# A graph layer's edge loop: its first eight blocks in another order, its store waits moved behind the barrier, and its last stage in one block with it

## What is computed

```python
pre_u = jnp.einsum('bud,dk->buk', h_t, W1[:d])
pre_v = jnp.einsum('bvd,dk->bvk', h_t, W1[d:])
hidden = jax.nn.relu(pre_u[:, :, None, :] + pre_v[:, None, :, :] + b1)
S = jax.nn.sigmoid(jnp.einsum('buvk,ko->buvo', hidden, W2)[..., 0] + b2[0])
a_t = jnp.einsum('buv,bud->bvd', S * A_a, h_t)
m_t = jnp.einsum('uv,bud->bvd', A_m, h_t) * h_t
z_t = beta1 * h_t + beta2 * (jnp.einsum('bvd,de->bve', a_t, Wa) + ba) + beta3 * (jnp.einsum('bvd,de->bve', m_t, Wm) + bm)
```

## Time and profile before

| | us |
|---|---|
| median of 3 runs | 3447.57 |
| lowest, highest | 3445.82, 3448.07 |
| profiled execution | 3449.29 |
| its span, first to last instruction | 3447.2 |
| TensorE busy | 3356.6 |
| VectorE busy | 2841.7 |
| ScalarE busy | 2342.5 |
| GpSimd busy | 1836.9 |

### The profile page before, as it was taken

One profiled execution on the slowest core, in us unless ns is written; L12 is line 12 of the kernel. 1 busy time (PEld: TensorE's weight loads), 2 busy tenths in 40 slices (PEclk: granted clock), 3 DMA queues, 4 the chain that ended last, 5 costly groups with the idle time before them and its releaser, 6 DMA issues. The chain is left out here.

```text
span 3447.2 us, 56125 instructions
## 1 busy us (share of the span) xinstructions
PE 3356.6 (97%) x14230; PEld 2618.5 (76%) x14230; DVE 2841.7 (82%) x4857; ACT 2342.5 (68%) x14070; POOL 1836.9 (53%) x2379
## 2 busy tenths in 40 slices
PE   7999999999998999999999999999999999689999
PEld 5667667676666888778878888878878888578888
DVE  5566765766547999999999999999999999469897
ACT  1222121221116999899999999999999999688997
POOL 3221221221114667656666676666666665578886
PEclk9999999999999999999999999999999999899999
DMA  7876777767669656775675666666656647587775
GB/s 273 296 262 240 264 255 247 284 248 256 230 205 225 155 122 165 165 171 139 139 174 132 176 137 159 171 152 153 168 141 168 155 114 189 183 285 249 263 257 193
DMA packets 345402, 685.80 MB, mean 199 GB/s; under 512 B 38990, under 2 KB 252856, under 8 KB 323512
## 3 DMA queue, kind: packets, MB, share of 16 engines
q1 hardware_dynamic: 289088, 594.50, 59.6%
q0 software_dynamic: 21504, 53.31, 5.0%
q10 hardware_dynamic: 34480, 34.34, 2.9%
HBM read 444.01 MB, written 256.18 MB: 203 GB/s over the span
## 5 line engine op out<-in xcount | busy, mean ns | idle before, releaser
L1240 ACT ACTIVATE junk<-psum_a 128x128 f32<-128x128 f32 x6144 | 1611.5, 293 | 199.0 <-PE psum_a L1144 110.2
L1240 ACT ACTIVATION_READ_ACCUMULATOR junk<-psum_a 128x1 f32 x6144 | 1367.8, 224 | 0.0
L1185 DVE TENSOR_REDUCE group_sum<-psum_d 128x56 f32<-128x896 f32 x1024 | 1111.5, 1085 | 87.8 <-PE psum_d L1144 42.0
L1144 PE MATMUL psum_d<-v_t,pk 128*128 128x512 f32 x1920 | 754.6, 393 | 0.0
L1292 POOL DMA_INDIRECT sum_dram<-total,idx_all x512 | 506.9, 990 | 228.3 <-POOL total L1303 124.1
L996 POOL TENSOR_TENSOR own<-whole 128x256 f32<-128x256 f32 x128 | 126.0, 985 | 753.9 <-DVE own_mixed L789 420.3
L1143 PE MATMUL psum_d<-u_t,pk 128*128 128x512 f32 x1280 | 503.9, 394 | 5.8 <-issue 4.7
L689 PE MATMUL wide<-shared,h 128*128 128x512 f32 x1024 | 482.2, 593 | 0.0
L747 ACT COPY whole<-ring 128x256 f32<-128x256 f32 x128 | 47.7, 373 | 630.4 <-PE ring L661 630.4
L1144 PE MATMUL psum_a<-v_t,pk 128*128 128x512 f32 x1152 | 453.4, 394 | 0.0
L1604 ACT ACTIVATE masked<-masked,of_u,half_sign 128x128 f32<-128x128 f32 x1024 | 399.7, 480 | 61.7 <-POOL masked L1541 61.7
(11 more groups left out here) (225 smaller groups left out, 5532.8 us busy)
## 6 DMA issues: line engine op xcount, KB each, us to landing
rows_dram<-split SPq DMA_DIRECT2D x128, 512.0 KB, 3.2
sum_dram<-zero SPq DMA_DIRECT2D x128, 512.0 KB, 4.0
u_t<-rows_dram SPq DMA_DIRECT2D x64, 1024.0 KB
shared<-sum_dram SPq DMA_DIRECT2D x64, 1024.0 KB, 6.3
first_u<-rows_dram SPq DMA_DIRECT2D x62, 1024.0 KB
pk<-pick_dram SPq DMA_DIRECT2D x448, 128.0 KB
whole_dram<-whole SPq DMA_DIRECT2D x128, 256.0 KB, 3.4
pick_dram<-first_v SPq DMA_DIRECT2D x128, 256.0 KB, 3.0
```

Source lines behind the costliest of these rows:

```text
L1144: return nc.tensor.matmul(dst, pk[n % PKS][:, SLOTS + at:SLOTS + at + P], part(v_t[n % VG][:], b, LB), start=False, stop=True)
L1185: nc.vector.tensor_reduce(out_[:, :, 1:EG], in_[:, :, GW:LATE].rearrange("p b (g k) -> p b g k", k=GW), AX, ALU.add, apply_absolute_value= ...
L1240: last = nc.scalar.activation(junk[:, a % RING_A, k * LATE:(k + 1) * LATE], psum_a[a % RING_A][:, k * LATE:(k + 1) * LATE], ACT.Abs, accum ...
```

## The change

1. **Store waits.** SP's waits for the first stage's stores are taken out of that stage. They stand, as `stage_stored`, at the start of the edge loop on SP, DVE, ACT and POOL (and of the multi-pass code); PE has none. All engines wait for `passes_made` instead, load `passes_i`, meet at the barrier, and branch over the multi-pass code, which now stands between first stage and edge loop.
2. **First blocks.** `steps` orders the first eight blocks as (u, v) = (0, 0), (0, 1), (1, 0), (1, 1), (0, 2), (0, 3), (1, 2), (1, 3). SP loads `v_t1`, `u_t1`, `v_t2`, `v_t3` in this order, and the third u-tile at n = 6 instead of n = 4.
3. **One block.** Edge loop and last stage are functions of one block: each engine goes from one into the other without a barrier. SP waits for all scatters and then loads; PE waits for all `drained`. `of_u` is finished on DVE after the second-last block.
4. **Work ahead.** The four adds of steps k = 0 and 1 are made by POOL after the scatters of blocks 251 to 254, into `masked_ahead`, which takes the place of the second `hWa` tile in `shared`. `adj_first` is loaded ahead too. `hWa_all[1]` is now the first load of the last stage.

```diff
@@ end of the first stage
-                    sp.wait_ge(linear_stored, 16 * 2)
-                    sp.wait_ge(own_stored, 16)
-                    sp.wait_ge(hWa_stored, 16 * B)
-                    sp.wait_ge(base_stored, 16 * B)
-                    for i in range(RPK):
-                        sp.wait_ge(pick_stored[i], 16 * ((PAIRS - i + RPK - 1) // RPK))
+                    sp.wait_ge(passes_made, 1)
...
+            passes = nc.values_load(passes_i[0:1, 0:1], min_val=0, max_val=PASSES)
             nc.all_engine_barrier()
@@ order and buffers
-        blocks = [(k % ST, (k - TURN * jj) // ST % NGRP * VG + jj) for k in range(ST * NGRP) for jj in range(VG)]
+        steps = [(0, 0), (0, 1), (1, 0), (1, 1), (0, 2), (0, 3), (1, 2), (1, 3)]
+        steps += [(k, jj) for k in range(2, ST * NGRP) for jj in range(VG)]
+        first_of = [min(n for n, step in enumerate(steps) if step[0] == k) for k in range(ST * NGRP)]
+        def block_at(k, jj):
+            return k % ST, (k - TURN * jj) // ST % NGRP * VG + jj
+        blocks = [block_at(*step) for step in steps]
-        hWa_ahead = [shared[:, i * ROW:(i + 1) * ROW].rearrange("p (b d) -> p b d", d=D) for i in range(RAW)]
+        hWa_ahead = shared[:, 0:ROW].rearrange("p (b d) -> p b d", d=D)
+        masked_ahead = [shared[:, ROW + i * P * B:ROW + (i + 1) * P * B].rearrange("p (b v) -> p b v", v=P) for i in range(RAW)]
@@ new: the waits for the stores
+        def stage_stored(eng):
+            eng.wait_ge(linear_stored, 16 * 2)
+            eng.wait_ge(own_stored, 16)
+            eng.wait_ge(hWa_stored, 16 * B)
+            eng.wait_ge(base_stored, 16 * B)
+            for i in range(RPK):
+                eng.wait_ge(pick_stored[i], 16 * ((PAIRS - i + RPK - 1) // RPK))
+            for i in range(RW):
+                eng.wait_ge(rows_stored[i], 32 * ((B * NT - i + RW - 1) // RW))
@@ SP in the edge loop
+                stage_stored(sp)
                 for n in range(1, PKS - 1):
                     load_pick(n)
-                    if n < VG:
-                        load_v(0, n)
+                    if n == 2:
+                        load_u(1)
+                    elif n in (1, 4, 5):
+                        load_v(0, max(n - 2, 1))
...
-                        if n % VG == 0 and n // VG + 1 < n_blk // VG:
+                    if n == 6:
+                        load_u(2)
+                    if n % VG == 0 and n >= 2 * VG and n // VG + 1 < n_blk // VG:
                         load_u(n // VG + 1)
...
                         for t in range(RAW):
                             sp.dma_start(raw[t], sum_uv[t * P:(t + 1) * P, 0:P, :]).then_inc(raw_loaded[t], 16)
-                            sp.dma_start(hWa_ahead[t], hWa_dram[:, t * P:(t + 1) * P, :].rearrange("b p d -> p b d")).then_inc(hWa_loaded[t], 16)
+                            sp.dma_start(adj_first[t][:], adj[t * P:(t + 1) * P, 0:P]).then_inc(adj_loaded[t], 16)
+                        sp.dma_start(hWa_ahead, hWa_dram[:, 0:P, :].rearrange("b p d -> p b d")).then_inc(hWa_loaded[0], 16)
@@ POOL in the edge loop
+                    if n >= n_blk - 5 and n < n_blk - 1:
+                        k, m = divmod(n - (n_blk - 5), 2)
+                        some = slice(m * HV, (m + 1) * HV)
+                        pool.wait_ge(raw_loaded[k], 16)
+                        pool.wait_ge(of_v_loaded[m], 16)
+                        pool.wait_ge(left_d, LD * LEFT)
+                        pool.wait_ge(left_a, LA * LEFT)
+                        TT(masked_ahead[k][:, :, some].rearrange("p b v -> p v b"), raw[k][:, some, :], of_v[:, some, :],
+                           ALU.add).then_inc(raw_added, 1)
+                for i in range(RING_S):
+                    pool.wait_ge(scattered[i], 16 * TILES * ((n_blk - i + RING_S - 1) // RING_S))
@@ the one block, here for SP; likewise PE, DVE, ACT and POOL
                 def _(sp):
+                    edges_sp(sp)
+                    last_sp(sp)
```

729 lines of the change are left out of this document (372 added, 357 removed).

## The result

| | before | after |
|---|---|---|
| median, us | 3449.06 (20 runs) | 3442.47 (20 runs) |
| lowest, highest | 3445.82, 3450.99 | 3438.56, 3447.23 |
| ratio, 95% interval | | 0.9982 (0.9976 to 0.9988) |
| profiled execution (its span) | 3449.29 (3447.2) | 3444.20 (3442.2) |

The account below looks back on a forecast made before the run. TensorE was taken to bound the edge loop's body, so gains could come only from the two ramps: 3449.3 - 11.4 (first blocks) - 4.0 (end) = 3433.9, less 1.7 for the median, said as 3432 us; range 3427.5 to 3439.

Parts of the forecast that it names:

- The chain and the body: Edge loop and last stage: TensorE bounds the body; the ninth raw tile sets k=8, 15.5 us later, then 389.67 us without waiting.
- First load 0.9 us earlier: Start of edge loop: with the store waits moved behind barrier and branch, SP's first load leaves at about 1028.2, 0.9 us earlier.
- Arrivals: First blocks: v_t1 lands at 1042.1, pick2 and u_t1 at 1053.7, v_t2 at 1065.4, v_t3 at 1076.6; block 8 starts at 1098.5.
- Block 8's u tile: First blocks: asked for after block 5, needs 11 to 13 us, there at 1096 to 1098, just in time; first-block gain 11.4 us.
- Rival 2: First blocks give half: late u tile holds block 8 3 or 4 us, or large loads come late; 3436 us; chance 0.12.
- both small: The end gives nothing and the first blocks give half, together 3440 us, at the edge of no change; chance 0.04.
- given back: Edge-loop body: first ramp's gain is lost because DVE or a left-over step is the real pace; 3443 to 3447; chance 0.04.
- The end, 4.0 us: Last ramp: the ninth raw tile comes 14.4 - 4.6 - 5.8 = 4.0 us earlier, bounds 0 to 6.
- the removed block end, barriers, register load, branch and adds, less the four adds ahead: End of edge loop: 14.4 us removed or done ahead, less 4.6 us by which POOL's adds delay the last scatter.
- the extra 2 MB: Last ramp: one more hWa tile (2048 KB) loaded ahead of all raw loads on a full DMA costs 5.8 us.
- The 1.7 us by which I lowered the forecast for the median: Whole kernel: median of the runs shown lay 1.7 us below the profiled execution, taking 3433.9 to 3432.2.
- the lower bound of 8 us for the first blocks: First blocks: gain of 8 us if the u tile takes the first load's 13.7 us and the start is not earlier.

Follow-up runs that it names:

- experiment 1: Changed kernel with the first gather of left-over rows issued after POOL's step of block 7 instead of block 4: 3430.64 us, ratio 0.9950.
- experiment 3: Kernel before with its first gather issued after POOL's step of block 2 instead of block 4: 3452.54 us, ratio 1.0019.
- experiment 6: Changed kernel with the 4-byte tile warm declared where it was, putting hWa tiles 32 bytes past a multiple of 64 again: ratio 0.9997.
- experiment 4: Changed kernel without the load of the second hWa tile (2048 KB) in the last ramp, so part of the output differs: 3439.38 us, ratio 0.9974.
- 5: Kernel of experiment 1 with 32 unused bytes per partition, edge-loop tiles back on multiples of 64: 3429.37 us, ratio 0.9949.
- 12: Kernel before with first_u and first_v right behind shared and warm; hWa tiles on 64, other edge tiles 32 past: 3444.53 us, ratio 0.9992.
- 9: Kernel 5 with first_u and first_v declared right behind shared and reused as hWa tiles 1 and 2, loaded in the ramp: 3421.31 us, ratio 0.9927.
- 13: Kernel 12 with 32 more unused bytes ahead of the edge loop's tiles, all of them on multiples of 64: 3437.12 us, ratio 0.9968.
- experiment 11: Kernel of experiment 1 with SP's store waits put back ahead of the barrier as well as behind it: 3430.94 us, ratio 0.9956.

## Why the prediction was wrong, point by point

**The chain and the body.** Right: the ninth `raw` tile sets the end, 15.5 us to k=8 and then 389 us; TensorE bounds the body, and what it loses at a block reaches the end.

**First load 0.9 us earlier.** Wrong, it is 0.0. The prediction added barrier, register load and branch on SP (they are short) and let the store land when it had landed before. The store lands 1.0 us later, in a stretch in which code loads run beside its end, and that is all of the gain. Measured from within the new program, the moved waits do save 1.4 us; the branch and the register load that now stand here cost as much.

**Arrivals.** The steps were right: from block 1 to block 8's turn 56.25 us against 56.4 worked out (1098.5 - 1042.1). All of it came 2.7 us later, 0.7 with the first stage, 0.9 with the first load, 1.25 with the first v tile, less 0.2.

**Block 8's u tile.** This is the step that failed: "needs 11 to 13 us: 1096 to 1098, just in time". The queue's own time was right (13.1 us in experiment 1). The step counted only what stands in SP's queue. POOL's gather of 4.0 MB, tied to block 4, left 16 us behind the u tile's issue in the kernel before (1092.1 against 1075.8), just as that tile's last bytes came (1092.4); in the new order block 4 comes earlier and the u tile later, and the gather runs 5.5 us ahead of it. Neither the code of the gather nor its queue is touched by the change, which is why it is not in the diff; in an order of POOL's instructions it stands unmoved. Rival 2 had the place and priced it at "3 or 4 us"; it was 11.3. I gave "both small" and "given back" 8 in 100 together, and it was neither's mechanism.
The Trainium skill ("DMA: Bandwidth & Descriptors", Queues, rings and completion order) says that a DMA engine goes in turn between the queues it has work for, and drains a packet of one before it goes to the next. The traces agree in that a second queue takes a share even of what was asked for earlier in the first: in experiment 3, with the gather asked for second, it had 56.1% of the engines from 1072 to 1080, against 39.7% for SP's queue. Even turns are not what the changed kernel shows: with the gather asked for first, it had 90.1% from 1088 to 1094, and SP's queue 10.4%. No run here says why the two differ.

**The end, 4.0 us.** The mechanism was right, and it brought 8.5. Term by term, by the way to k=8:
- the removed block end, barriers, register load, branch and adds, less the four adds ahead: 14.4 - 4.6 = 9.8 worked out, 9.58 measured (from the last edge matmul to the first ramp load 22.37 before, 12.79 after). Four adds took 2.37 to 2.46 us (2.40 forecast), and DVE and TensorE were not held:

```profile
2949.12 2.46 POOL L1510 TENSOR_TENSOR shared<-shared,of_v 128x1024 f32<-128x1024 f32 x1
...
2956.89 2.37 POOL L1510 TENSOR_TENSOR shared<-shared,of_v 128x1024 f32<-128x1024 f32 x1
```

- the extra 2 MB: 5.8 worked out; with the tiles placed as before 5.0 (experiment 6: 98.58 - (103.19 - 9.58)), as placed now 4.05 (experiment 4). That is less than its bytes at the ramp's own rate (2.1 MB at 386 GB/s are 5.4 us), and no run says what the rest is;
- the place of the `hWa` tiles: nothing in the prediction; 3.9 us (experiment 6 against the changed kernel).

With the old placement the end would have given 4.6 us. So nearly half of what the end brought, and more than half of all that the change brought, is an alignment that nobody asked for.

**The sum.** 15.4 us were forecast, and 5.0 stand between the two profiles: 11.3 lost at block 8, 2.15 at the first loads, 1.6 in the first stage and the body, 0.2 gained in the order, 4.5 gained at the end (15.4 - 11.3 - 2.15 - 1.6 + 0.2 + 4.5 = 5.05). The 1.7 us by which I lowered the forecast for the median came from three executions; over the twenty the profiled one lies only 0.2 us above the median. And the lower bound of 8 us for the first blocks does not follow from its terms: a u tile asked for at 1086.1 that takes 13.7 us is there at 1099.8, which leaves 10.1 us.

**The range and the chances.** The range left out the case that a transfer of another queue meets the late tile, though its row could have been found: POOL's gather stood in the timeline, and the earlier trace rows shows that I read POOL's timeline at the end of the loop only. With this one number changed (experiment 1) the time is 3430.6, which the forecast of 3432 would have met, but partly by luck, with an error at the start and another at the end that cancel.

## What to carry to other kernels

When an edit moves a load later or a block earlier, list every transfer of every queue in the stretch between issue and need, also those of engines that the edit does not touch, and ask of each what its trigger does now; a load that was asked for first does not come first if another queue is filled beside it. A wait moved behind a barrier and a branch buys the overlap only if what then runs, code loads too, is not on the same DMA engines as what is waited for. Before a gain is put down to a reordering, compare the addresses of the tiles in both programs: here a 4-byte tile declared elsewhere was worth 3 to 4 us in loads, and two tiles laid elsewhere, with 32 bytes of padding, 7 to 8 us in the time.

## What the runs showed of the hardware that I had not expected

- Loads in packets of 1 KB into tiles that lie 32 bytes past a multiple of 64 in their partition ran slower than into tiles on a multiple: the ramp moved 367 and 368 GB/s (kernel before, experiments 3 and 6) against 381 to 387 in the eleven others. For loads that ran near 220 GB/s in packets of 16 KB no such difference was seen (experiments 5 and 12).
- The pace of the same matmuls, at full clock and busy alike, depended on where the tiles lie: from block 8 to the last edge matmul 1838.4 and 1839.1 us against 1829.5 and 1830.7 (pairs 5 and 9, 12 and 13). The cause is open.
- A 1 MB store whose end fell together with five code packets (0.05 MB) landed after 5.4 us (changed kernel, experiment 1), without them after 4.4 (kernel before, experiment 11).
- A gather of 4.0 MB in POOL's queue, asked for 5.5 us ahead, made a 2 MB load in SP's queue take 24.6 us in place of 13.1 (changed kernel, experiment 1); the load's first packet of 16 KB passed after 5.7 us in place of 1.4.
- The other way round, the gather's first packets passed 6.8 and 7.1 us after it was asked for where SP's queue kept the engines full (experiments 3 and 1), and 1.8 us after in the kernel before and in the changed one.
